# Half of the query rotations moved from ahead of the causal attention's scores to between its softmax steps

## The reference, cut to what matters

```python
q = (x @ Wq).reshape(b, t, H, D).transpose(0, 2, 1, 3)
ckv = x @ Wkva
kv_latent, k_rope = (ckv[:, :, :R], ckv[:, :, R:])
...
q_nope, q_rope = (q[..., :NOPE], q[..., NOPE:])
q = jnp.concatenate([q_nope, _rope(q_rope)], axis=-1)
k = jnp.concatenate([kv, _rope(k_rope)], axis=-1)
att = jnp.einsum('bhqd,bhkd->bhqk', q, k) / jnp.sqrt(jnp.float32(D))
att = jax.nn.softmax(jnp.where(mask, att, jnp.float32(-jnp.inf)), axis=-1)
y = jnp.einsum('bhqk,bhkd->bhqd', att, v)
```

## Time and profile before

| what | value |
|---|---|
| median of three runs | 783.92 us |
| the profiled execution | 782.88 us |
| its span | 781.1 us |
| TensorE busy with matmuls | 711.4 us, 91% of the span |
| VectorE busy | 490.2 us, 63% |
| ScalarE busy | 379.0 us, 49% |
| GpSimd busy | 220.6 us, 28% |
| pairs turned on VectorE | from 242.9 to 266.0 us |
| softmax steps, first to last shift | from 269.8 to 315.2 us |

### The profile page before, as it was taken

How to read it: one execution, slowest core, us unless ns; L and a number is a source line. 1 busy time by engine, 2 the same in 40 slices (tenths; PEclk the granted TensorE clock), 3 DMA queues, 4 the chain that set the end, 5 groups by cost and what they waited for, 6 DMA issues and landing times.

```text
span 781.1 us, 13394 instructions
## 1 busy us (share of the span) xinstructions
PE 711.4 (91%) x4735; PEld 596.4 (76%) x4735; DVE 490.2 (63%) x956; ACT 379.0 (49%) x820; POOL 220.6 (28%) x238
## 2 busy tenths in 40 slices
PE   6999999999989699998998999998993799999996
PEld 3578888889955588577995576676773699999995
DVE  3266666665328799466657667777777465666662
ACT  4513233323362289554434466565766165656561
POOL 0006765555400043600003411114000322334232
PEclk9999999999999899998999999999996699999999
DMA  6500000000072200000000878436052388999972
GB/s 231 233 1 21 20 20 20 20 1 1 1 293 100 79 3 1 1 1 1 0 11 33 179 175 193 116 98 183 25 213 85 111 299 279 331 298 325 302 217 60
DMA packets 31441, 89.45 MB, mean 115 GB/s; under 512 B 4201, under 2 KB 20841, under 8 KB 28049
## 3 DMA queue, kind: packets, MB, share of 16 engines
q1 hardware_dynamic: 27537, 83.36, 32.9%
q0 software_dynamic: 3840, 5.25, 3.3%
HBM read 74.74 MB, written 10.38 MB: 109 GB/s over the span
## 4 chain that ended last, share of the span: by engine, by line
PE 75%; DVE 14%; ACT 4%; issue 4%; DMA 3%; POOLq 0%; SPq 0%; DVEq 0%; ACTq 0%
PE PS L514 71%; DVE SM L2124 2%; PE PS L1096 2%; PE PS L685 1%; DMA XB<-token_rows,XROW 1%; DVE RB L1879 1%; DVE SM L1791 1%; DVE RQ L1881 1%; DVE PROD L1774 1%; PE PS L1066 1%; DVE KTHL L2086 1%; PE PS L913 1%; ACT SQ L1141 1%; DVE RW L1787 1%; ACT RO L1271 1%
## 5 line engine op out<-in xcount | busy, mean ns | idle before, releaser
L514 PE MATMUL PS<-CTXH,WKV0H 128*128 128x362 f32 x256 | 86.4, 338 | 3.8 <-DVE PROD L1774 3.2
L514 PE MATMUL PS<-CTXH,WKV0L 128*128 128x362 f32 x256 | 84.0, 328 | 0.0
L514 PE MATMUL PS<-CTXL,WKV0H 128*128 128x362 f32 x256 | 84.0, 328 | 0.0
L2124 DVE TENSOR_REDUCE SM<-PS 100x1 f32<-100x362 f32 x128 | 64.5, 529 | 30.5 <-PE PS L514 29.7
L1397 ACT ACTIVATE WK<-PS 120x400 f32<-120x400 f32 (+1 forms) x96 | 48.3, 508 | 39.9 <-PE PS L514 39.2
L1813 DVE TENSOR_TENSOR RW<-PS,RW 128x400 f32<-128x400 f32 x64 | 36.8, 574 | 47.4 <-ACT RW L1207 33.7
L1207 ACT COPY RW<-PS 128x361 f32<-128x361 f32 x64 | 29.6, 463 | 65.0 <-PE PS L514 52.5
L1670 POOL DMA_INDIRECT out<-YO,TROW x20 | 33.0, 1649 | 96.8 <-DMA out<-YO,TROW 69.5
L514 PEld LDWEIGHTS PS<-CTXH,WKV0H 128*128 128x128 f32 x256 | 48.1, 188 | 12.8 <-DVE PROD L1774 6.5
L514 PE MATMUL PS<-KST,QST 97*100 97x362 f32 x128 | 51.4, 412 | 5.4 <-DVE SM L2124 4.2
L514 PE MATMUL PS<-RB,HTT 114*128 114x256 f32 (+1 forms) x240 | 55.2, 379 | 0.6 <-ACT HTT L1509 0.6
(11 more groups left out here) (326 smaller groups left out, 1813.6 us busy)
## 6 DMA issues: line engine op xcount, KB each, us to landing
RB<-W SPq DMA_DIRECT2D x14, 1368.0 KB, 6.6
RB<-W SPq DMA_DIRECT2D x20, 768.0 KB
KST<-keys_by_head SPq DMA_DIRECT2D x24, 362.0 KB
RQ<-W SPq DMA_DIRECT2D x6, 1368.0 KB
keys_by_head<-KTHL SPq DMA_DIRECT2D x8, 724.0 KB, 3.6
CTX<-ctxT SPq DMA_DIRECT2D x16, 361.0 KB, 7.0
RB<-WK SPq DMA_DIRECT2D x16, 200.0 KB, 2.2
RW<-WGU SPq DMA_DIRECT2D x1, 2304.0 KB, 8.5
```

What stands on the lines that cost most here:

```text
L514: return pe.matmul(out, lhsT, rhs, start=start, stop=stop)
L2124: dve.tensor_reduce(SM1[:, q % 2, j:j + 1], PS[0:S, i % 2, 0:KVE], AX_X, ALU.max, negate=True).then_inc(sem["c_maximum_found"], 1)
```

## The change

TensorE's `qk(0)` waits for four turned pairs only, and `qk(8)`, the first of batch 4, for all eight. VectorE turns pairs 0 to 3 and takes cosines 4 ahead of the softmax loop; the other sines and cosines stand in the loop, behind the shift of a step and in front of the division of the step before: sines 4, 5, 6, 7 in steps 0, 2, 4, 6 and cosines 5, 6, 7 in steps 1, 3, 5. `SH` moves to the region of the squares, since `PT0` is now written while pairs are still being turned. The instructions and transfers are otherwise the same ones.

```diff
-        SH = cut(RB, 9536, 1600).rearrange("p (s c) -> p s c", s=4)
+        SH = cut(SQF, 0, 1600).rearrange("p (s c) -> p s c", s=4)
...
                     pe.wait_ge(sem["b_latent_rotated"], 6)
+                    pe.wait_ge(sem["b_query_rotated"], 4)
+                if i == B:
                     pe.wait_ge(sem["b_query_rotated"], 8)
...
-            for j in range(9):
-                if j < 8:
-                    cosines(j)
+            for j in range(5):
+                cosines(j)
                 if j:
                     sines(j - 1)
...
             for i in range(2 * B + 1):
                 if i < 2 * B:
                     shift_b(i)
+                if i < 7 and i % 2 == 0:
+                    sines(4 + i // 2)
+                if i < 6 and i % 2 == 1:
+                    cosines(5 + i // 2)
                 if i:
                     divide_b(i - 1)
```

## The result

The changed kernel takes 786.99 us, the median of 19 runs, against 783.83 us for the kernel before on the same chips: a ratio of 1.0055, 95% interval 1.003 to 1.008. Run again later beside several experiments, it gave a ratio of 1.004 (1.0007 to 1.0072). It is slower by 2 to 6 us: 3.2 us by the medians, 4.3 us by the means, from which the ratio is taken. Single executions of either kernel scatter over several us; the four longest of the 19, 793.8 to 794.6 us, had a mean clock of 0.957 to 0.958 on TensorE, the other fifteen 0.967 to 0.970. Without those four the ratio of the means would be 1.0034; no trace shows where they lose their 7 us. The stage itself can be read more finely in the traces than the totals allow.

A forecast was written before the change was run, and what follows sets the result against it. VectorE was taken to bound the softmax's first half: -5.70 us earlier start, +10.41 moved turning, -0.72 filled idle give +3.99; TensorE's surplus takes 0.8 off, +3.2. 783.92 + 3.2 = 787.1 us; own range 786.3 to 788.6, 8 in 10 785.0 to 789.3.

The forecast's parts named there:

- The start of the scores: qk(0) at 262.10 us, VectorE's first reduction 5.70 us earlier; as a rival, that gain stays: 778.2 us, chance 0.08.
- The 1.62 us of clock within the 5.70: In qk(0): at full clock it takes 1.94 us instead of 3.56, part of the earlier first reduction.
- The moved turning: VectorE idles 8.93 us before the first scores, then does 10.41 us of turning; step 7's shift comes 3.99 us late.
- The second half: From step 7, VectorE goes at 2.90 us a step, TensorE at 3.05; step 15's reduction comes 3.2 us late.
- The 0.8 us that the surplus gives back: Steps after 7: TensorE's surplus of 0.15 us a step swallows part of the delay, 3.99 to 3.2 us.
- Edits at no cost: In the softmax: qk(8)'s wait for sines 7, swaps 6 and 7 released later, and SH's new place add nothing.
- The total: Whole kernel: 3.2 us slower, 787.1 us as the median of the runs.
- The forecast's own range: Whole kernel: 786.3 to 788.6 us, for unknown terms of 0.3 us between the pace's ends and 0.8 for SH.
- my price of up to 1.6 us around steps 7 to 9: Rival: TensorE's clock falls in the thinned loop; one or two spells there or in the tail, 788.7 to 790.3; chance 0.12.
- Rival 3: Low clock spell at 318 us, after the softmax, is missed: 1.6 us back, 785.5 us; chance 0.15.
- the case of two spells: Two later low clock spells gone: 783.9 us, no change; within the same rival's chance of 0.15.
- the row of 4.62 us: TensorE's wait before qk(0), after the latent is summed, until VectorE turns the last pair; cited as speaking for a rival.

The follow-up runs named there:

- the kernel with the wait alone: Kernel before with only TensorE's wait split, qk(0) after four turned pairs and qk(8) after eight, VectorE's order untouched: ratio 0.9947, median 779.02 us.
- the block experiment: Changed kernel, but VectorE waits for the first scores, then turns pairs 4 to 7 in one block, nothing interleaved: ratio 1.0087 to the kernel before.
- two pairs on GpSimd: Kernel before with the wait split, SH at its new place, and sines 6 and 7 done by GpSimd instead of VectorE: ratio 0.9949.

## Why the prediction was right

**The start of the scores.** 262.10 was predicted, 262.05 measured; `qk(0)` took 1.97 us, and the first reduction came at 264.04 against 264.06. The release by the copy of the latent was the right next wait. The 1.62 us of clock within the 5.70 were had in the profiled executions of the changed kernel, but in the kernel with the wait alone they were not, in the same place; that term is a matter of the execution.

**The moved turning.** Idle 8.80 us (8.93 predicted), a sines 1.93 us of the stream, a cosines 0.90; steps of 3.8 and 4.8 us in turn; the eighth reduction at 293.46, 0.01 from the figure.

**The second half.** VectorE goes at 2.90 up to the reduction of step 13, TensorE's chain starts at 296.67 (296.66 predicted) and decides at 316.93. The 0.8 us that the surplus gives back came as worked out.

**Edits at no cost.** The place is shown to be free by itself. No reduction and no sines waited for a swap. `qk(8)` was held by sines 7, as computed, until 292.27, 1.15 us of idle time on TensorE that nobody felt.

**The total.** +3.2 us predicted, +3.16 between the medians; the interval of the ratio, +2.4 to +6.3 us, would also have covered 5. The forecast's own range, 786.3 to 788.6, does not follow from the two terms given for it: 0.3 and 0.8 us to either side of 787.1 make 786.0 to 788.2. Nothing hangs on it. The agreement of the total is partly luck: the profiled execution was 4.4 us longer. That of the stage is not.

**The rivals.** The start of the scores is worth nothing by itself: where VectorE keeps its order, 4 us of it arrive; where it idles, none. The clock did fall in the loop in one of two traces of the changed kernel, as the rule of the Trainium skill ("TensorE: Matmul & The Clock Gate", "A second HAM failure mode: psum-queue depth-cycling") warned; my price of up to 1.6 us around steps 7 to 9 was too high at least for step 7, where VectorE covered all of it. A clock under 1.00 between 264 and 314 us stood among my signs of being wrong; it came, and the steps kept their length. The price of a low spell where VectorE does not cover it is in the block experiment: 1.61 us of the 2.22. Rival 3, the later spell going away, happened in that same second execution, 1.69 us back. So did the case of two spells: one that the kernel before has from 543 us is gone too. The span of that execution is 782.5 against 781.1 us, 1.4 us longer, though its sixteenth reduction lies 4.0 us behind. In the first execution the spell had only moved along. The 3.2 us are thus shown for the stage; the total of a single execution carries such spells besides.

What I left unsaid was the better half: the row of 4.62 us was a real loss, and the wait alone takes it back.

## What to carry to other kernels

Before moving work out from in front of a wait, ask what its engine will do in that time instead. If the engine also sets the pace behind the wait, work that leaves the waiting time is not hidden but postponed: the loss comes from the engine's new idle time, and it can be read off the order of the instructions. Here that is 8.8 us, of which 7.2 are left at the end of the stage against the kernel with the wait alone. Relax the wait first and leave the order alone; then fill only the pause that remains, 0.6 us here, with a single sines.

## What the runs showed of the hardware

**The clock after a short pause differs between executions.** In two executions of the changed kernel TensorE paused for 1.40 and for 1.39 us in the same place; it fell to 1.2 GHz in the first (0.50 from 322 us) and stayed at 2.4 GHz in the second. After 0.46 us of idle time behind the same matmuls it stayed at 2.4 GHz in the changed kernel and fell to 1.2 GHz within the microsecond from 262 in the kernel with the wait alone; after 2.46 us, in the one execution of that kernel, it was low. A measured saving that rests on the clock needs more than one trace.

**Some instructions of GpSimd and VectorE shut each other out.** A VectorE product of two operands in SBUF took 2.67 us beside a GpSimd product of 2.26, instead of 0.98; a `TENSOR_SCALAR` of four columns took 1.06 instead of 0.17 and ended at 266.12, GpSimd's product at 266.10. A reduction that reads PSUM took its 0.98 beside the same product, and one of 100 x 400 elements that reads SBUF (268.87 us, two pairs on GpSimd) took 0.55 beside GpSimd's addition, as it does alone (0.56). The Trainium skill, "SBUF — State Buffer", section "SBUF: two separate sides", describes an exclusive lock on a port pair shared by the two, held for a whole instruction; the ends that coincide agree with it. GpSimd's instruction grew too: 2.26 and 2.50 us beside VectorE's product, 1.87 and 1.88 later.
